# Info and mask kept in four strips of 32 partitions and replicated in full fp32, with a shorter dependent chain for inverse roots

## The reference

```python
# block 1, on the group-normed image (groups of two channels)
info = relu(info_w @ x + info_b)            # 16 rows
mask = sigmoid(mask_w @ x + mask_b)         # 16 rows
expanded[m*16 + i] = mask[m] * info[i]      # 256 rows
x = x + relu(out_w @ expanded + out_b)
# block 2, tokens layer-normed: linear attention (elu + 1), 8 heads, then an MLP, two more layer norms
# block 3, tokens layer-normed: 8 experts of 128 hidden units, the two best of a softmax gate
t = t + sum_e cw[e] * (gelu(t_n @ W1[e] + b1[e]) @ W2[e] + b2[e])
```

## Time and profile before

| | |
|---|---|
| median of 3 runs | 1252.85 us (1252.8 to 1252.86) |
| the profiled execution | 1252.97 us, its span 1251.2 us |
| PE busy | 1092.2 us (87%) |
| DVE busy | 852.6 us (68%) |
| ACT busy | 699.9 us (56%) |
| GpSimd busy | 362.2 us (29%) |
| mean granted TensorE clock | 0.978 |
| the chain that ended last | PE 58%, DVE 25%, ACT 12%, issue 4%, DMA 1% |

### The profile page before, as it was taken

How to read it: one execution, slowest core, us unless ns; L and a number is a source line. 1 busy time by engine, 2 the same in 40 slices (tenths; PEclk the granted TensorE clock), 3 DMA queues, 4 the chain that set the end, 5 groups by cost and what they waited for, 6 DMA issues and landing times.

```text
span 1251.2 us, 14277 instructions
## 1 busy us (share of the span) xinstructions
PE 1092.2 (87%) x5238; PEld 501.4 (40%) x5238; DVE 852.6 (68%) x1751; ACT 699.9 (56%) x960; POOL 362.2 (29%) x276
## 2 busy tenths in 40 slices
PE   4776598979899799988989899997989979999897
PEld 2454244423544244442454334542444424534232
DVE  5656766697658876488585876669665887646433
ACT  3443365664665645755646656556466565566454
POOL 0100031233313423134313333124331333313466
PEclk8888699999999999999999999999999999999999
DMA  2110392008610094003920058100861019300570
GB/s 103 34 34 1 75 202 63 1 18 180 145 34 18 21 219 108 11 18 78 215 65 1 18 125 199 34 1 17 183 142 34 18 32 220 73 1 18 124 167 34
DMA packets 15797, 96.39 MB, mean 77 GB/s; under 512 B 2992, under 2 KB 5104, under 8 KB 11504
## 3 DMA queue, kind: packets, MB, share of 16 engines
q1 hardware_dynamic: 15728, 95.49, 32.7%
HBM read 77.66 MB, written 9.44 MB: 70 GB/s over the span
## 4 chain that ended last, share of the span: by engine, by line
PE 58%; DVE 25%; ACT 12%; issue 4%; DMA 1%; POOL 0%; DVEq 0%; POOLq 0%; SPq 0%; ACTq 0%
PE HP L647 10%; PE HP L662 9%; PE R L518 7%; PE R L586 5%; PE R L477 4%; PE R L488 4%; PE R L470 4%; DVE T L983 3%; PE R L532 3%; DVE TM L1100 2%; ACT H L788 2%; DVE SM L956 2%; PE R L561 2%; PE R L593 2%; PE R L662 2%
## 5 line engine op out<-in xcount | busy, mean ns | idle before, releaser
L828 POOL TENSOR_TENSOR XB<-TM,XB 128x512 f32<-128x512 f32 x256 | 324.8, 1289 | 825.2 <-DVE TM L1100 825.2
L788 ACT ACTIVATE H<-HP,W 128x1024 f32<-128x1024 f32 x224 | 237.7, 1114 | 98.9 <-PE HP L647 97.8
L647 PE MATMUL HP<-XF,W1E 64*128 64x512 f32 x1024 | 256.8, 620 | 25.5 <-DVE TM L1100 24.6
L662 PE MATMUL HP<-H,W 128*64 128x512 f32 x896 | 226.2, 611 | 29.1 <-ACT H L788 29.1
L1100 DVE SCALAR_TENSOR_TENSOR TM<-HP,B2S,CWB 128x512 f32<-128x512 f32 x224 | 159.4, 742 | 105.7 <-PE HP L662 102.1
L647 PEld LDWEIGHTS HP<-XF,W1E 64*128 64x128 f32 x1024 | 87.8, 186 | 150.4 <-DVE TM L1100 79.3
L956 DVE TENSOR_REDUCE SM<-T 128x8 f32<-128x512 f32 x128 | 86.3, 685 | 50.7 <-ACT T L725 49.3
L662 PEld LDWEIGHTS HP<-H,W 128*64 128x64 f32 x896 | 49.0, 135 | 176.9 <-ACT H L788 133.8
L725 ACT ACTIVATE T<-R 128x512 f32<-128x512 f32 x128 | 74.7, 597 | 79.1 <-PE R L518 77.7
L932 DVE SCALAR_TENSOR_TENSOR BIG<-R,T 128x512 f32<-128x512 f32 x128 | 79.8, 683 | 33.7 <-PE R L470 33.3
L488 PE MATMUL R<-W,T 128*128 128x128 f32 x512 | 78.0, 296 | 19.9 <-DVE T L975 19.0
(11 more groups left out here) (117 smaller groups left out, 1417.8 us busy)
## 6 DMA issues: line engine op xcount, KB each, us to landing
CWB<-gates_hbm SPq DMA_DIRECT2D x32, 1536.0 KB, 20.4
CWB<-gates_hbm SPq DMA_DIRECT2D x32, 512.0 KB, 6.7
X<-x SPq DMA_DIRECT2D x16, 512.0 KB, 6.5
BIG<-XN SPq DMA_DIRECT2D x32, 256.0 KB, 3.9
out<-XB SPq DMA_DIRECT2D x16, 512.0 KB, 2.7
W<-wpack SPq DMA_DIRECT2D x1, 1176.0 KB, 7.0
gates_hbm<-CWR SPq DMA_DIRECT2D x16, 64.0 KB, 1.6
W1E<-w1e SPq DMA_DIRECT2D x1, 512.0 KB, 8.4
```

The lines of the kernel that those rows point to most:

```text
L647: last = mm(HP[u % BATCH][:, half(k)], W1E[img(k), e, :], XF[img(k), 1 - par, s, half(c)], start=True, stop=True)
L662: last = mm(sums_of(b, u)[img(k), :], w("w2e")[:, C * e:C * e + C], activated(b, u)[:, k, :], start=True, stop=True)
L788: f(activated(b, u).rearrange("p k t -> p (k t)"), HP[u % BATCH][:, :], ACT.Gelu, bias=col(B1E + e))\
L828: nc.gpsimd.tensor_tensor(acc, TM[:, u % BATCH, :], acc, ALU.add).then_inc(acc_done, 1)
```

## The change

Info and mask now lie in four strips of 32 partitions: `strip(kind, s, c)` is strip `2 * (s ^ kind) + c`, with kind 0 for info and 1 for mask. PE computes 32 rows at a time into the strip of its kind and piece, all in the first 512 columns of `R[s]` (4 matmuls for a slot, in place of 2), and signals once for a slot. ACT applies relu to 64 partitions (both halves of the slot) and tanh to 64, straight into `IM`, so two instructions for a slot in place of four. DVE's rounding and difference are gone. A replication matmul reads one strip of 32 partitions of `IM` and the same strip of `REP`, both fp32. `REP` and the biases `BI` are loaded into the strips by 16 small DMAs in place of one.

`rsqrt` keeps the half of the value times the guess in `hy` and refines `hy` and `y` by the same factor, so a refinement is one product and two multiplications that depend on it alone. `count` signals without a wait. There are 11 instructions in a chain, as before, and 9 waits in place of 11.

`SCHEDULE` is another one: six batches of a group are left over at `first_unit`, where there were eight.

```diff
-    ("group_norm", "Y"), ("choose_1", ""), ("info_mask_0", "HY"), ("choose_2", "HY"), ("info_mask_1", "H"),
-    ("gate_rows", "Y"), ("info_0.0", ""), ("info_0.1", "H"), ("low_0.0", ""), ("low_0.1", "Y"),
+    ("group_norm", ""), ("choose_1", ""), ("info_mask_0", "YH"), ("choose_2", ""), ("info_mask_1", "Y"),
+    ("gate_rows", "H"), ("info_0.0", ""), ("info_0.1", "YH"), ("low_0.0", ""), ("low_0.1", "Y"),
...
-        IM = sb("IM", [P, G, T], F32R)
+        IM = sb("IM", [P, G, CH])
...
+            for q in range(4):
+                there = slice(32 * q, 32 * q + 32)
+                sp.dma_start(by_image(REP[there, :, :])[:, :, 0, :], rep[0:32, :, 0, :]).then_inc(r_in, 16)
+                sp.dma_start(by_image(REP[there, :, :])[:, :, 1:3, :], rep[32:64, :, 1:3, :]).then_inc(r_in, 16)
+                for kind in range(2):
+                    sp.dma_start(BI[there, kind, :], im_bias[32 * kind:32 * kind + 32, :]).then_inc(bi_in, 16)
...
-                    for c in range(NCH):
-                        mm(R[s][img(c), half(c)], w("wim"), XN[:, s, half(c)], start=True, stop=True)\
-                            .then_inc(im_ps, 1)
+                    for kind in range(2):
+                        for c in range(NCH):
+                            last = mm(R[s][strip(kind, s, c), 0:CH], w("wim")[:, 32 * kind:32 * kind + 32], XN[:, s, half(c)],
+                                      start=True, stop=True)
+                    last.then_inc(im_ps, 1)
...
-                            pe.wait_ge(hl_done, nth(a + 1, s, c))
+                            pe.wait_ge(im_act, nth(a + 1, s))
...
-                        mm(R[s][:, half(c)], REP[:, n, :], IM[:, s, half(c)], start=True, stop=True).then_inc(rep_ps[s], 1)
+                        rows = strip(1 if n % 3 else 0, s, c)
+                        mm(R[s][:, half(c)], REP[rows, n, :], IM[rows, s, :], start=True, stop=True).then_inc(rep_ps[s], 1)
...
-                        f(T1[0:32, s, half(c)], R[s][info, half(c)], ACT.Relu, bias=col(B_IM, info))
-                        f(T1[32:64, s, half(c)], R[s][mask, half(c)], ACT.Tanh, bias=BT[mask, :], scale=0.5)\
-                            .then_inc(im_act, 1)
+                    info, mask = img(s), img(1 - s)
+                    f(IM[info, s, :], R[s][info, 0:CH], ACT.Relu, bias=BI[info, 0, 0:1])
+                    f(IM[mask, s, :], R[s][mask, 0:CH], ACT.Tanh, bias=BT[mask, :], scale=0.5).then_inc(im_act, 1)
...
-                    for _ in range(3):
-                        link(v.tensor_tensor(t, y, y, ALU.mult))
-                        link(v.tensor_tensor(t, t, hz, ALU.mult))
+                    link(v.tensor_tensor(hy, hz, y, ALU.mult))
+                    for last in (False, False, True):
+                        link(v.tensor_tensor(t, hy, y, ALU.mult))
+                        if not last:
+                            count(v.scalar_tensor_tensor(out=hy, in0=t, scalar=-1.5, in1=hy, op0=ALU.add, op1=ALU.mult))
                         link(v.scalar_tensor_tensor(out=y, in0=t, scalar=-1.5, in1=y, op0=ALU.add, op1=ALU.mult))
...
-                        high = IM[0:C, s, half(c)]
-                        v.tensor_copy(high, T1[0:C, s, half(c)]).then_inc(hl_high, 1)
-                        dve.wait_ge(hl_high, nth(a + 1, s, c))
-                        v.tensor_tensor(IM[C:P, s, half(c)], T1[0:C, s, half(c)], high.bitcast(F32),
-                                        ALU.subtract).then_inc(hl_done, 1)
```

More of the change, by code:

```diff
@@ L133, in build @@
         B2S = sb("B2S", [P, 2, EP])
-        REP = sb("REP", [P, NREP, P], F32R)
+        REP = sb("REP", [P, NREP, P])
+        BI = sb("BI", [P, 2, 2])
         ST = sb("ST", [P, G, 32])
@@ L180, in build @@
         r_in = sem("r_in")
+        bi_in = sem("bi_in")
         e_in = sem("e_in")
@@ L299, in activated, with strip @@
             return HR[u % FREE] if last_group(b) else H[:, u % BATCH, :, :]
+        def strip(kind, s, c):
+            q = 2 * (s ^ kind) + c
+            return slice(32 * q, 32 * q + 32)
         def gt(k):
@@ L695, in _ @@
             act.wait_ge(w_in, 16)
-            f(BT[:, :], col(B_IM), ACT.Copy, scale=0.5).then_inc(act_prep, 1)
-            act.wait_ge(r_in, 16)
-            f(REP[:, :, :], raw_reps.rearrange("p (n c) -> p n c", c=P), ACT.Copy).then_inc(act_prep, 1)
+            act.wait_ge(bi_in, 128)
+            f(BT[:, :], BI[:, 1, 0:1], ACT.Copy, scale=0.5).then_inc(act_prep, 1)
             act.wait_ge(act_prep, 1)
@@ L702, in info_mask @@
                 def info_mask(s):
-                    for c in range(NCH):
-                        act.wait_ge(im_ps, nth(a + 1, s, c))
-                        info, mask = slice(C * c, C * c + 32), slice(C * c + 32, C * c + 64)
-                        f(T1[0:32, s, half(c)], R[s][info, half(c)], ACT.Relu, bias=col(B_IM, info))
-                        f(T1[32:64, s, half(c)], R[s][mask, half(c)], ACT.Tanh, bias=BT[mask, :], scale=0.5)\
-                            .then_inc(im_act, 1)
+                    act.wait_ge(im_ps, nth(a + 1, s))
+                    info, mask = img(s), img(1 - s)
+                    f(IM[info, s, :], R[s][info, 0:CH], ACT.Relu, bias=BI[info, 0, 0:1])
+                    f(IM[mask, s, :], R[s][mask, 0:CH], ACT.Tanh, bias=BT[mask, :], scale=0.5).then_inc(im_act, 1)
                 def info(k, slots):
@@ L858, in parts, with count, link @@
                 steps = {chain: 0, router: 0}
-                def link(ins, signal=chain, per_group=CHAIN_STEPS):
+                def count(ins, signal=chain):
                     steps[signal] += 1
                     ins.then_inc(signal, 1)
+                def link(ins, signal=chain, per_group=CHAIN_STEPS):
+                    count(ins, signal)
                     dve.wait_ge(signal, a * per_group + steps[signal])
@@ L872, in rsqrt @@
                     span = slice(slots[0], slots[-1] + 1)
-                    hz, t, y = (SM[:, k, span, 0:n] for k in (1, 2, 3))
+                    hy, hz, t, y = (SM[:, k, span, 0:n] for k in range(4))
                     link(v.tensor_scalar(y.bitcast(I32), hz.bitcast(I32), -0.5, RSQRT_GUESS, ALU.mult, ALU.add))
-                    for _ in range(3):
-                        link(v.tensor_tensor(t, y, y, ALU.mult))
-                        link(v.tensor_tensor(t, t, hz, ALU.mult))
+                    link(v.tensor_tensor(hy, hz, y, ALU.mult))
[3 more added lines that the diff above has]
+                            count(v.scalar_tensor_tensor(out=hy, in0=t, scalar=-1.5, in1=hy, op0=ALU.add, op1=ALU.mult))
                         link(v.scalar_tensor_tensor(out=y, in0=t, scalar=-1.5, in1=y, op0=ALU.add, op1=ALU.mult))
```

18 lines of the change are left out of this document (7 added, 11 removed), and 20 rows, old and new, of the table SCHEDULE.

## The result

The changed kernel takes 1246.18 us in the median (1245.67 to 1246.97, 4 runs) against 1252.86, a ratio of 0.9944 with a 95% interval of 0.9927 to 0.9961. The forecast was 1223 us, with a range of 1203 to 1246. The sign was right, the size was a fifth of it, and the time lies at the upper end, just outside. The profiled execution took 1246.97 us, its span 1245.2.

What follows compares the result with a forecast made beforehand. PE, with holes in the routing region behind DVE's queue, bounds steady turns. Six steady turns 17.4, first turn 3, second 1 and the end 8.7 make 30 us off 1252.97, so 1223 us; range 1203 to 1246.

Steps and rivals of the forecast that it cites:

- What bounds the kernel: Steady turns: PE bounds them, with 13.9 us of holes, 6.5 in the routing region, where DVE is the late engine.
- DVE's work removed, 3.5 us a turn: Routing region: L921 and L923 go, 5.6 us of DVE a group; holes shrink from 6.5 to 3.4 us, 3.5 gained.
- the 3 us that the prediction named as a sign against it: Routing region: first layers that still wait 3 us would show the forecast wrong.
- The replication, +1.2 us a turn: Replication stage: strips overlap at 1.0 us per group of four, 7.9 us in place of 7.7, plus 1.0 of lateness.
- the conflict of `low_1.0` and `info_1.1`: Replication stage: both want the same two strips, so their group takes two rounds, 1.9 us.
- The inverse roots, -0.6 us a turn: Five chains a turn: each shortens by 0.3 us, experts cover most of it in steady turns, 0.6 us gained.
- The steady turns, -2.9: Six steady turns: -3.5 + 1.2 - 0.6 = -2.9 us each, -17.4 in all; a period of 145 us, not 148.
- First turn, -3, and second turn, -1: First: roots -1.5, earlier inputs -3.5, 2 given back. Second: DVE -4.5, roots -1.5, two more batches +5.
- The second turn's +5 us for two more batches: Second turn: the new schedule adds two batches, 7.7 us of PE, which fill the 25.2 us of holes only in part.
- The end, -8.7: Behind the last dense turn: 22 batches run in place of 24, at 4.36 us each, 8.7 us less.
- (c): Replication: strips overlap in pairs only, 11.8 us in place of 7.9, +31 in 8 turns, 1254 us, no change; chance 0.05.
- (d): Replication: strip matmuls run one after another, 23.5 us, +125 in 8 turns, 1348 us, slower; chance 0.09.

Runs made afterwards that it cites:

- second probe: Changed kernel with fp32 matmuls without waits put ahead on PE: 16 single strips, 16 pairs, 16 threes, 10 fours; one run, 1328.8 us with the block.
- the two probes: Changed kernel with wait-free fp32 matmuls ahead on PE: four-strip groups and full-array matmuls (1299.6 us), or one to four strips at a time (1328.8 us).

## Why the prediction was wrong

**What bounds the kernel.** Right. PE with holes bounds the steady turns, the holes lie in the routing region, and DVE's row makes them.

**DVE's work removed, 3.5 us a turn.** The length was right, the mechanism in part. The region came to the 24.0 us that were worked out, but the first layers wait 2.7 us for the combine as they had (2.9), near the 3 us that the prediction named as a sign against it; the holes that went are the second layers'. And the sum treated the gain as the removal's own, where it is that of the removal and of the new places of the first layers together: in steady turns the schedule alone costs 2.0 us, since its first layers wait behind L921 and L923 and the clock falls in that hole, and the strips alone cost 1.5. The prediction priced both as one, so for the whole this did no harm.

**The replication, +1.2 us a turn.** A size. Strips overlap, a group of four takes 1.14 us (the next work starts 1.07 us behind its start) where 1.0 was taken, and PE's replication went from 7.7 to 9.6 us, +1.9, which is 0.7 too little in the forecast. The number of groups (seven) and the conflict of `low_1.0` and `info_1.1` (1.99 us) were as read from the order.

**The inverse roots, -0.6 us a turn.** Undersized. A chain takes 1.97 us from the guess on in place of 2.21, 0.24 less, where 0.3 was said; but experts cover nothing of it: alone it gave 1.3 us a steady turn, as much as five chains, 0.7 more than forecast.

**The steady turns, -2.9.** The turns of 145.1 and 145.3 us hit it, and that is luck in part: replication was 0.7 us dearer than forecast and the roots gave 0.7 more. The others take 146.7 or 146.8. In those the clock falls for 3.4 us at the end of the region with the holes, which no steady turn of before showed. I had given these turns no risk from the clock.

**First turn, -3, and second turn, -1.** This is the step that failed: they came to +5.9 and +9.7. I wrote that "a strip group takes 2 us, just what three other products of DVE cover", gave back 2 us in the first turn, and put nothing in the second. It prices strips in groups of four, with the lower clock lasting no longer than the 6.8 us of before. Both premises were wrong. At that clock the strips run in pairs, not in fours, and a pair takes 1.71 us (second probe), so the twelve pairs of a stage make 20.5 us (an estimate from the two) and PE, not DVE, sets the pace: the stage took 21.9 us. And the low clock lasted through all of it and into `conv_out`, and through 18.8 us of the second stage.

What the form costs at each clock, in the first turn's stage:

| | mostly or all at the full clock | all at the lower clock |
|---|---|---|
| fp32r on 128 rows | 14.6 (before, 6.8 us of it low) | 15.8 (roots alone) |
| fp32 strips | 14.9 (filled) | 21.9 (the changed kernel) |

At the full clock the strips cost next to nothing, at the lower one 6.1 us. How long the clock stays low is not fixed by the form. Fp32r had it up again 8.5 us into the first stage before, and 3.2 us into the second, but not at all in the first stage with the roots alone. Unfilled strips had it high for 7 us in the first stage of the strips alone, and lost it. In the second turn the wait ahead of the stage got 5.0 us shorter, where 4.5 were taken, and the stage 15.1 longer: 5.2 of it also with the schedule alone, 9.9 with the strips on top. That the low clock with the strips is the cause, and not the chain of products as such, was shown by filling the idle strips: 6.3 us of the first turn came back with more work on PE, and 9.7 of the whole. The second turn's +5 us for two more batches was near: the schedule alone gives +6.0.

**The end, -8.7.** Right: with the last steady turn it is -11.7 against -11.6.

**The rivals.** None came in the steady turns. (c), strips that overlap in pairs only, is what happened in the early ones, at the lower clock: its argument, that replication depends on DVE's pace, was sound there, and its answer, "most groups stand behind expert work", doesn't hold where there are no experts. It was priced at the full clock, 0.98 us a pair. (d), no overlap at all, came nowhere. I excluded both by rows at the full clock, where the stages in question start at the half one. The earlier trace rows had shown the danger.

What stays open: why the holes of the routing region let the clock fall in some steady turns and not in others, which is worth 1.6 us a turn; how much of the 14.9 us of the filled first stage is due to the clock being high at its start; and when unfilled strips get the clock up, after 12.2 us in one profile of the second stage and after 18.8 in another. The stages' figures rest on one profiled execution of each kernel, the gain by filling on the medians too.

## What to carry to other kernels

A form of matmul is priced at the clock of the place where it runs: here the same exchange cost 0.3 us at the full clock and 6.1 at the lower one. It can also change that clock. Before a full-array operation is replaced by strips, look at what brought the clock up in the trace of before, and whether the new form will run with all its strips at once or piece by piece behind its inputs. And parts that were changed together should be priced together: two that each made the kernel slower gave back nearly all of it once both were in.

## What the runs showed of the hardware

- Single row strips and pairs, fp32 and without a pause, ran 54 us at the lower clock; three side by side were at the full one some 4 us after they began, four 4.4 us after (the two probes). In the kernel, unfilled strips lost the full clock after 7 us without a pause of PE (strips alone).
- Four fp32 matmuls on four row strips of 32 rows took 0.87 us a group in a long row, as long as one on 128 rows (13.14 us for 15). At the lower clock a record lasts 1.056 us in place of 0.587.
- A group of strips ends as late as its last piece and one whole fp32 matmul: 1.96 us in place of 1.14 where one piece started 0.8 us late.
- Two DVE instructions on 128x32 of which the second doesn't wait for the first start 0.11 us apart, where a linked one starts 0.22 to 0.23 after the one before:

```profile
55.26 0.19 DVE L896 SCALAR_TENSOR_TENSOR SM<-SM 128x32 f32<-128x32 f32 x1
55.37 0.18 DVE L897 SCALAR_TENSOR_TENSOR SM<-SM 128x32 f32<-128x32 f32 x1
55.59 0.19 DVE L894 TENSOR_TENSOR SM<-SM 128x32 f32<-128x32 f32 x1
```
